# A new order of work inside each expert of a mixture-of-experts layer, with other banks for two products and another engine for the expert tiles

## The reference, cut to what matters

```python
probs = jax.nn.softmax(x_tokens @ router_w + router_b, axis=-1)      # 16 experts
vals, idx = jax.lax.top_k(probs, 2)
vals = vals / (vals.sum(-1, keepdims=True) + 1e-9)
# every expert takes at most C = 640 token rows, in order of arrival
expert_inputs = zeros((16, C, 512)).at[idx_flat, pos_c].add(x_pair)
expert_outputs = vmap(lambda h, wg, wu, wd: silu(h @ wg) * (h @ wu) @ wd)(expert_inputs, w_gate, w_up, w_down)
gathered = expert_outputs[idx_flat, pos_c] * (vals_flat * within)[:, None]
return x + _mlp(x, sw_gate, sw_up, sw_down) + gathered.reshape(N, 2, d).sum(axis=1)
```

## Time and profile before

| | us |
|---|---|
| median of 3 runs | 1927.52 |
| the runs | 1926.8 to 1929.26 |
| the profiled execution, whole | 1925.47 |
| its span | 1923.8 |
| PE busy | 1810.9 (94%) |
| DVE busy | 1243.3 (65%) |
| POOL busy | 1054.0 (55%) |
| ACT busy | 889.0 (46%) |

### The profile page before, as it was taken

The page is one execution under the profiler, slowest core; times in us unless marked ns, Lnnn a source line. Parts: engine busy times, 40 slices in busy tenths (PEclk is TensorE's granted clock), DMA queues, the critical chain, the costliest instruction groups (busy, mean ns, idle before and its releaser), DMA issues.

```text
span 1923.8 us, 27307 instructions
## 1 busy us (share of the span) xinstructions
PE 1810.9 (94%) x9689; PEld 1595.2 (83%) x9689; DVE 1243.3 (65%) x2579; ACT 889.0 (46%) x1638; POOL 1054.0 (55%) x809
## 2 busy tenths in 40 slices
PE   9999999999999999999998998899889988998897
PEld 6888888888878888888888888888788888888887
DVE  6677777778644444437675777567666766686663
ACT  5465556564643333315454445344534553554341
POOL 3444546556442222246657755775577557755861
PEclk9999999999999999999999999999999999999999
DMA  9354555443423332245547555654575456546642
GB/s 330 117 143 130 133 144 148 147 140 103 116 37 44 45 78 45 44 101 132 103 133 165 122 100 140 156 125 101 135 160 118 106 142 151 114 115 146 145 86 28
DMA packets 236007, 229.35 MB, mean 119 GB/s; under 512 B 169664, under 2 KB 169920, under 8 KB 234592
## 3 DMA queue, kind: packets, MB, share of 16 engines
q1 hardware_dynamic: 210432, 174.50, 33.4%
q0 software_dynamic: 25440, 53.11, 15.7%
HBM read 138.80 MB, written 49.97 MB: 98 GB/s over the span
## 4 chain that ended last, share of the span: by engine, by line
PE 50%; DVE 16%; POOL 14%; issue 9%; ACT 6%; DMA 4%; POOLq 0%; SPq 0%; DVEq 0%; ACTq 0%
PE ps L73 31%; PE ps L2111 8%; PE ps L2140 7%; POOL out_tokens L1570 6%; POOL buffer L1528 5%; ACT buffer L1618 4%; PE ps L1003 3%; DMA buffer<-in_wts 3%; DVE buffer L1804 2%; DVE ps L1855 2%; POOL buffer L1533 1%; DVE buffer L1812 1%; DVE buffer L1936 1%; ACT buffer L1670 1%; PE ps L1147 1%
## 5 line engine op out<-in xcount | busy, mean ns | idle before, releaser
L73 PE MATMUL ps<-buffer,buffer 128*128 128x512 f32 (+1 forms) x4596 | 912.1, 357 | 33.1 <-DVE buffer L1913 32.4
L73 PEld LDWEIGHTS ps<-buffer,buffer 128*128 128x128 f32 x4596 | 785.9, 188 | 143.6 <-DVE buffer L1913 36.6
L1618 ACT ACTIVATE buffer<-buffer 128x512 fp32r<-128x512 f32 (+7 forms) x555 | 379.5, 736 | 245.2 <-DMA buffer<-in_wts 148.3
L2140 PE MATMUL ps<-buffer,buffer 128*128 128x512 f32 (+1 forms) x1921 | 439.1, 389 | 3.1 <-DVE buffer L1848 3.1
L2140 PEld LDWEIGHTS ps<-buffer,buffer 128*128 128x128 f32 x1921 | 357.9, 188 | 77.1 <-issue 3.7
L2111 PE MATMUL ps<-buffer,buffer 128*128 128x320 f32 x2016 | 341.6, 333 | 64.5 <-ACT buffer L1618 63.3
L2111 PEld LDWEIGHTS ps<-buffer,buffer 128*128 128x128 f32 x2016 | 332.4, 209 | 69.8 <-ACT buffer L1618 67.3
L1528 POOL TENSOR_TENSOR buffer<-buffer,buffer 128x512 fp32r<-128x512 f32 x176 | 260.3, 1729 | 26.2 <-ACT buffer L1618 26.2
L1533 POOL TENSOR_TENSOR buffer<-buffer,buffer 128x768 fp32r<-128x768 f32 x48 | 89.6, 1866 | 237.8 <-ACT buffer L1618 237.3
L521 POOL DMA_INDIRECT slots<-pairs,slot_u x64 | 63.5, 992 | 209.1 <-DVE slot_u L990 192.0
L1570 POOL DMA_INDIRECT out_tokens<-buffer,slot_list x79 | 130.0, 1645 | 55.7 <-DVE buffer L1936 32.5
(11 more groups left out here) (162 smaller groups left out, 1865.8 us busy)
## 6 DMA issues: line engine op xcount, KB each, us to landing
buffer<-in_wts SPq DMA_DIRECT2D x128, 512.0 KB, 3.7
buffer<-in_wts SPq DMA_DIRECT2D x33, 256.0 KB, 3.5
buffer<-in_xT SPq DMA_DIRECT2D x8, 1024.0 KB, 5.5
buffer<-in_ctxT SPq DMA_DIRECT2D x8, 1024.0 KB, 8.0
out_tokens<-buffer SPq DMA_DIRECT2D x8, 1024.0 KB, 4.3
tokens_normed<-buffer SPq DMA_DIRECT2D x32, 256.0 KB, 2.9
out_tokens<-buffer POOLq DMA_DIRECT2D x32, 256.0 KB, 6.7
buffer<-in_x SPq DMA_DIRECT2D x7, 1024.0 KB, 5.7
```

What stands on the lines that cost most here:

```text
L73: last = pe.matmul(out, left, right, start=(c == 0 and i == 0), stop=(c == len(parts) - 1 and i == 2))
L1618: return act.activation(dst, src, ACT.Copy)
L2140: ins = pe.matmul(down_bank[(n + i) % 2][:, part_cols], left, right, start=(c == 0 and k == 0), stop=(c == FC - 1 and k == len(passes) - 1))
```

## The change

On PE the order of matmuls stays; their waits and banks change. On the other four engines the loop over experts is rewritten in single steps, in a new order.

- **Banks.** The third bank of a plain unit is gone: the product goes back into the gate bank. 0A uses ps 0 and 1, 0B and 4B use ps 3 and 6, 4A uses the two down banks, 5A one down bank, 5B `ps[1]`. Pairs 1 and 3 have (0, 1, 2), pair 2 has (3, 6, 7), in every expert.
- **Buffers.** `third_sum` is two buffers instead of one; `hh`, `hl` and the silu buffers move by a quarter of a row.
- **Tiles.** An expert's down tiles are taken out of PSUM by ACT (a Copy with the gate as scale), no more by DVE. The shared tiles stay on DVE.

PE's waits, which replace `set_free`:

```diff
+        def bank_free(e, what):
+            if what in ("0A", "0B", "m15", "m25") and e == 0:
                 pe.wait_ge(s_hl, len(units))
+            elif what == "0A":
+                pair_silu_ready(pe, e - 1, "a", 3)
+                low_ready(pe, e - 1, 5, 1)
+            elif what == "0B":
+                low_ready(pe, e - 1, 4, 1)
+            elif what == "m11":
+                low_ready(pe, e, 0, 0)
+            elif what == "m16":
+                product_ready(pe, e, 0, 0)
+            elif what == "m15":
+                pair_silu_ready(pe, e - 1, "b", 3)
+            elif what == "m21":
+                low_ready(pe, e, 0, 1)
+            elif what == "m26":
+                product_ready(pe, e, 0, 1)
+            elif what == "m25":
+                pair_silu_ready(pe, e - 1, "b", 2)
+            elif what == "m31":
+                pair_silu_ready(pe, e, "a", 1)
+            elif what == "m36":
+                low_ready(pe, e, 1, 0)
+            elif what == "m35":
+                pair_silu_ready(pe, e, "b", 1)
+            elif what == "4A":
+                pe.wait_ge(s_ost, tiles_before[B + e])
+            elif what == "4B":
+                pair_silu_ready(pe, e, "a", 2)
+                low_ready(pe, e, 2, 0)
+            elif what == "5A":
+                product_ready(pe, e, 4, 0)
+            elif what == "5B":
+                low_ready(pe, e, 3, 0)
+            elif what == "d0":
+                low_ready(pe, e, 4, 0)
+            elif what == "d1":
+                low_ready(pe, e, 5, 0)
```

The tile steps on ACT and the plain unit on DVE:

```diff
+        def evict(e, t):
+            g = B + e
+            n = tiles_before[g] + t
+            act.wait_ge(s_add[t], 16 * adds_of(g, t))
...
+            gate = slot_list[:, e * ET + t, 1:2]
+            for i, cols in enumerate(column_parts(g, t)):
+                act.wait_ge(s_down, n + i + 1)
+                act.activation(ost[:, t, cols], down_bank[(n + i) % 2][:, cols], ACT.Copy, scale=gate).then_inc(s_ost, 1)
...
-            dve.wait_ge(s_silu, plain_count(e, c, j))
-            dve.tensor_tensor(z_bank[0:rows_of(c), 0:EH], y_bank[rows, 0:EH], esilu[0:rows_of(c), :], ALU.mult)\
-               .then_inc(s_ht, 1)
+            plain_silu_ready(dve, e, c, j)
+            dve.tensor_tensor(gate[0:rows_of(c), 0:EH], up[rows, 0:EH], esilu[0:rows_of(c), :], ALU.mult).then_inc(s_ht, 1)
```

More of the change, by code:

```diff
@@ L1269, in phase2, with numbered @@
[L1269 to L1281, removed]
+    def numbered(first, steady):
+        number = {}
+        for name in first.split():
+            number[name, 0] = len(number) + 1
+        for e in range(E):
+            for name in steady.split():
+                of = e + name.endswith("+")
+                if of < E:
+                    number[name.rstrip("+"), of] = len(number) + 1
+        return number
@@ L1283, in pair_no, with pair_before, plain_banks @@
     def pair_no(e, c):
         return NP * e + PAIRED.index(c)
[L1286 to L1290, removed]
+    def pair_before(e, c, k):
+        n = pair_no(e, c) - k
+        return n // NP, PAIRED[n % NP]
+    def plain_banks(e, c, j):
+        a = tiles_before[B + e] % 2
+        if c == FC - 1:
+            return [(down_bank[1 - a], down_bank[1 - a]), (ps[1], ps[1])][j]
+        if (c, j) == (4, 0):
+            return down_bank[a], down_bank[1 - a]
+        return (even_banks, odd_banks)[j][0:2]
@@ L1300, in product_count @@
[L1300 to L1308, removed]
     FIRST = WC - 1
@@ L1583, in gpsimd @@
                 pool.wait_ge(s_list, 16)
-                gather(0)
+                for t in range(ET):
+                    gather(0, t)
             for c in range(FC):
@@ L1989, in vector @@
                     pair_sums(0, PREPARED[g, c])
-            if g == B - 1:
-                tokens_and_tiles(g, 0)
-            else:
+            if g < B - 1:
                 for t in range(NT):
                     evict(g, t)
+        for t in range(ET - 1):
+            x_low(0, t)
+        evict(B - 1, 0)
+        x_low(0, ET - 1)
+        x_sums(0, 0)
+        x_sums(0, 2)
+        evict(B - 1, 1)
+        x_sums(0, 1)
+        x_sums(0, 3)
+        x_lo(0, 0)
+        evict(B - 1, 2)
+        x_lo(0, 1)
+        x_sum_lo(0, 0)
+        evict(B - 1, 3)
+        for i in (2, 1, 3):
+            x_sum_lo(0, i)
+        last_rows()
         for e in range(E):
@@ L2038, in vector @@
                 pair_sums(e + 1, 2)
-            tokens_and_tiles(B + e, e + 1)
+                x_low(e + 1, 0)
+                x_low(e + 1, 1)
+                x_low(e + 1, 2)
+                x_low(e + 1, 3)
+                x_low(e + 1, 4)
+                x_sums(e + 1, 0)
+                x_sums(e + 1, 2)
+                x_sums(e + 1, 1)
+                x_sum_lo(e + 1, 0)
+                x_sums(e + 1, 3)
+                x_lo(e + 1, 0)
+                x_lo(e + 1, 1)
+                x_sum_lo(e + 1, 2)
```

640 lines of the change are left out of this document (348 added, 292 removed).

## The result

The changed kernel takes 1791.6 us in the median of 4 runs (1791.3 to 1792.51) against 1927.52: ratio 0.929, 95% interval 0.928 to 0.931. The forecast was 1812 with a range from 1794 to 1850. The nearest of the rivals was A, by which the new chains never touch PE.

The account below looks back on a forecast made before the run. PE, 94% busy, was held by two waits and a low clock. Experts 1 to 14 fall from 64.79 to 57.0 us (109), expert 15 gains 6.2, expert 0 none: 115 off 1925.5, plus 2.0, gives 1812 us; range 1794 to 1850.

Parts of the forecast that it names:

- A: Rival: the new chains never touch PE, period 56.0 to 56.4 us, time 1799 us; chance 0.21.
- What bounded the kernel: PE's waits of 4.22 and 2.03 us and 2.65 us of low clock per expert; without them 55.9 us.
- Part 1, the ring: Weight loads: piece 5 done at T + 5.5, long wait before product 22 and low clock go; 6.87 us an expert.
- Part 2, the banks: 4B's up bank moves to ps 6 of pair 2, so its wait of 2.03 us goes.
- Part 3, the tiles: Five evictions per expert go from DVE to ACT; neither engine is the bound, tile 0's chain hidden by 1.4 us.
- Part 4, POOL's load: POOL's work per expert is 49.6 us, 89% of a 55.9 us period; it just fits.
- Part 5, the new waits: Three chains with little in hand cost between 0 and about 4 us an expert; 1.1 taken.
- (a): DVE's sums wait for load 1 before lo 1A, wanted at product 36; cost 0 to 0.5, up to 1.5 us.
- (b): `third` 3 stands behind `pair_sums(n,1)` on DVE, wanted by product 34; cost 0 to 0.8 us.
- (c): Token work at the turn of an expert: x_lo due at T + 55.9, lo 0A at T + 7.04; 0 to 1.5 us.
- Expert 0: First expert: 2.4 us of the short wait goes, late piece 9 costs about 2.5 us; net gain 0.
- C: Rival: POOL keeps its old timing, PE waits 8 us at product 36, time 1953 us; chance 0.06.

Follow-up runs that it names:

- run 4: Changed kernel with 4B back in the banks of pair 3, its up bank waiting for low part 3A, and 5B in ps 3; 1815.0 us.
- run 11: Changed kernel with pieces 5 to 7 copied by ACT after silu and hi of 0A again; 1786.7 us.
- run 1: Changed kernel with POOL's low parts of pieces 3 and 4 of the next expert ahead of all five scatters again; 1865.3 us.
- run 6: Kernel before the change, with only POOL's low part of piece 5 moved ahead of the previous expert's five scatters; 1983.8 us.
- run 2: Changed kernel with the experts' tiles taken out of PSUM by DVE again, placed in DVE's new order; 1814.6 us.
- run 3: Changed kernel with the experts' tiles on DVE in its new order, tile 1's eviction after three of DVE's five token copies; 1811.5 us.
- run 5: Kernel before the change, with only the new order of weights on ACT and POOL; banks, DVE's order and DVE's tiles stay; 1881.0 us.
- run 7: Kernel before the change, with the new order of weights and the experts' tiles on ACT, placed as in the changed kernel; 1825.4 us.
- run 9: Changed kernel with tokens turned after load 3, row operations later, and POOL's shared adds ahead of the low parts of pieces 2 to 4; 1791.1 us.
- run 10: Changed kernel with tokens turned after load 3, row operations later, POOL's shared adds first, pieces 2 to 4 held until DVE's x_sum_lo are done; 1786.6 us.
- run 8: Changed kernel with expert 0's tokens turned after load 3 and the two small row operations at the end of expert 0; 1786.8 us.
- run 12: Changed kernel with ACT's pieces 5 to 7 late, tokens turned after load 3 and row operations at the end of expert 0; 1784.6 us.

## Why the prediction was wrong in size and right in mechanism

**What bounded the kernel: right.** The two waits and the low clock were the whole gain. Their sizes were 4.22, 2.03 and 2.65; the last was too small. Both pieces of block products took 8.98 + 10.57 = 19.55 us from start to start before and 16.72 now, 2.83 less, and the short wait had cost PE another 0.26 around it (run 4: 0.25). So the period without them is 55.4, not 55.9: 7.5 us over 14 experts.

**Part 1, the ring: right.** Piece 5 was due at T + 5.5; the run of six that holds it (after piece 4) begins at T + 3.3, so piece 5 is done at T + 6.0. Product 22 no longer waits. ACT's slack for piece 5 was not used up (run 11), POOL's was the one that counts (runs 1 and 6).

**Part 2, the banks: right** in mechanism. In the new order the bank alone is worth 23 us (run 4), the new orders had the rest.

**Part 3, the tiles: no wait came, but their worth was missed.** No term of the sum depends on them, so they have no share in the miss. But the working asks only whether both engines have time for them, by their busy shares and one chain, and not what DVE would delay if it kept them. Runs 2 and 3 show 16 to 23 us in the finished order; runs 5 and 7 show 56 on the way to it, together with the move of ACT's token copies. A busy share does not say where an engine's few microseconds stand: at the turn of an expert DVE had none.

**Part 4, POOL's load: right** in that it fits (42.6 of 55.4 us busy, and gaps between DMA issues), too dark in the price of one low part: 1.66 and 2.52 instead of 1.75 and 2.81. Its 49.6 us were too many for the old order already, whose window shows POOL busy for 43.22 of 64.51 us.

**Part 5, the new waits: the step that failed.** Its term of 1.1 us an expert for three chains was too large: they cost nothing, 15.4 us over 14 experts. Here are the rows in which they end (T is 1226.34; L1909 begins the sums, L2018 is lo 1A, L1984 `third` 3, L1940 the two x_lo); PE wants them at T + 18.6, 27.3 and 55.4:

```profile
1241.95 0.41 DVE L1909 TENSOR_TENSOR buffer<-buffer 128x256 f32<-128x256 f32 x1
...
1243.61 0.49 DVE L2018 TENSOR_TENSOR buffer<-ps,buffer 128x320 fp32r<-128x320 f32 x1
...
1251.87 0.48 DVE L1984 TENSOR_TENSOR buffer<-ps,buffer 128x320 f32<-128x320 f32 x1
...
1278.43 2.89 DVE L1940 TENSOR_TENSOR buffer<-buffer,buffer 128x1280 fp32r<-128x1280 f32 x2
```

(a): the sums start at once and lo 1A is done at T + 17.8. (b): `third` 3 is done at T + 26.0. (c): the first of the two x_lo is done by about T + 53.6, and lo 0A at T + 6.0 against 7.0. Each had 0.8 to 1.8 us in hand. Two things made the term. The bounds came from durations that belong to the old neighbours: 0.91 us for the first subtraction of a pair's sums, which takes 0.42, and up to 3.02 (1.92 in the median) for a low part that takes 0.82 when POOL is not subtracting beside it. And the 1.1 between the bounds was taken from two short waits of expert 0, for `plain_product` and `second`, which are none of the three chains.

By the Trainium skill, page "SBUF — State Buffer", section "Who interferes with whom", it is the order of issue and not the shape of the operations that decides who is blocked. Runs 9 to 11 agree in that the same three operations took 10.11, 2.29, and 2.79 us with POOL's run against them, behind them, or stopped. They do not show the rest: in run 9 the held operation began, by the profile, at 888.1, 0.2 us before POOL's run (starts on POOL are rough), and it was held for the whole run of six and not for one instruction. The prediction took the rule as speaking against the change. At the places that PE waits for it spoke for it, since the new order puts POOL's scatters, and not its subtractions, beside DVE's low parts; the token copies, which have time, got the subtractions.

**Expert 0: wrong.** The sum had 0; it lost 5.7 us. Chain (a), expected there, was hidden behind something earlier: lo 0A was 4.64 us late, behind 5.00 us of blocked low parts and 2.35 of two tiny row operations that the change had moved there, beside the same subtractions, and the tokens were turned after loads 4 and 5, an edit that the prediction did not price. Runs 8, 11 and 12 show these causes. The difference to the forecast closes: 7.5 + 15.4 + 1.5 (expert 15) - 5.7 + 0.2 = 18.9 us, against 134.1 - 115.2. The medians lie 20.4 apart. The rest is the 2.0 us added for the step from the profiled execution to the median, which was 0.15 after the change (1791.45 and 1791.6), less rounding.

**Rivals.** C lives, in two forms: run 1 (with part of its price) and run 6 (slower than the kernel before). It did not happen, since the scatters had indeed gone ahead.

## What to carry to other kernels

When a wait in a chain of loads is removed, ask for the next load of the same ring before counting the gain: one move gave 56 us the wrong way, the full order with the evictions on ACT 102 the right way. Take durations for a new order only from rows where the neighbour engine does what it will do then; a median over the old neighbours can be more than double. And price the first turn of a loop apart from the steady one: it has other neighbours, and here it held all that runs 8 to 12 could still win.

## What the runs showed of the hardware

One DVE subtraction of 128x640 with both inputs in SBUF took 0.82 us alone and up to 8.64 while POOL ran six subtractions back to back. DVE's 16-bit copies from SBUF to SBUF took 0.45 us alone and 1.5 in the mean beside POOL's subtractions (7.55 for five), while scatters and adds issued by POOL left the low parts alone (0.82 in the median beside scatters, 2.29 for three during the last of the adds). ACT took a 128x512 bank out with a scale in 0.68 us, DVE in 0.74.

The granted clock after a wait of PE was 1.00 behind the waits of 1.8 to 2.5 us inside 4B, 0.89 over the 15.7 us behind one of 2.52, 1.00 over the 5.4 us behind one of 3.12 and 0.75 over the 6.9 us behind one of 3.30, and 0.65 over the 7.9 us behind one of 8.10. How much a wait of 2.5 to 3.3 us costs beyond itself is thus not settled by its length here.
